# Attention tower kernel: attention tiles of 128 tokens, the 513th query and key apart on quarters of the partitions

## The chip, the cores and the metric

The kernel runs as one program on one core of a Trainium2 chip. The metric is the device time of one execution in microseconds. A profile of one execution shows when each engine worked: TensorE (PE; its weight loads are the rows PEld), VectorE (DVE), ScalarE (ACT), GpSimd (POOL) and the queues that issue transfers (SP).

## The reference, cut to what matters

The whole program is a small tower for 4 images of 513 tokens (512 and a class token) with 192 channels. Two of its layers are softmax attention with 12 heads of 16 channels; the rest (token features, a state-space mixer, MLPs, a mixture of experts, a spiking layer) is not touched by the change. For each image and head both layers compute

```python
qkv = (xp @ w_qkv).reshape(B2, N, 3, H, hd).transpose(2, 0, 3, 1, 4)   # N = 513, H = 12, hd = 16
a = jax.nn.softmax(jnp.einsum('bhnd,bhmd->bhnm', q, k) * scale, axis=-1)
o = jnp.einsum('bhnm,bhmd->bhnd', a, v)
```

513 is one more than four times 128, and 128 is the number of partitions and of TensorE rows and columns.

## The kernel before, in words

An attention layer (`attention_layer`, called for `att0` and for `att1`) has three stages: `qkv` makes queries, keys and values, `attention` does the softmax sums, `heads_out` projects. Before, 513 tokens were cut in five tiles (`KT`): four of 104 and one of 97.

`qkv` goes over 20 tiles (4 images by 5). Per tile TensorE projects queries and keys (L1817, 384 columns, float32), then values (L1822, 192 columns, float32), and turns 12 blocks of the result so that channels lie on partitions (L1839). ScalarE and VectorE split the projections in float16 parts and copy the turned blocks to `q2` and `kT`.

`attention` goes over 12 groups (4 images by 3 sets of four heads). The four heads of a group are numbered by `gi` (0, 1) and `e` (0, 1); heads with e=0 lie on partitions 0 to 63, those with e=1 on 64 to 127, so two matmuls of 64 rows can run side by side. A group needs, first, the maximum over the keys for each query:
- *scores* (L1982): 20 matmuls (2 gi, 5 tiles of queries, 2 e), each tile against 512 keys, into three PSUM banks in turn (`ring`). VectorE reduces each bank to a maximum (L2068).
- *last keys* (L1993): 10 small matmuls with the 513th key, which VectorE joins to the maxima (two operations, L2079).
- *turn* (L2004): 10 transposes that put the maxima in one row; VectorE copies the row of e=0, ScalarE that of e=1, into `q2` (L1936, two copies of 513 numbers each), where the next matmuls subtract it.

Then the softmax sums, with the keys on the partitions:
- *keys* (L2027): 20 units (2 halves of 257 queries, 5 tiles of keys, 2 gi), each a pair of matmuls (e=0 and 1) into one of two pairs of banks, and one Exp on ScalarE for each unit (L2103, 514 elements a partition).
- *values* (L2043): for each tile of keys four float32 matmuls, one for each head, side by side on quarters of 32 columns; the trace shows each as two records. ScalarE copies the sums of a half away (L2092).

TensorE's order is written by hand: a step is keys, a pair of scores, keys, and the values of two steps earlier. A group has 10 steps. The scores run `LEAD = 13` steps ahead, so those of the first group and part of the next stand alone at the start of the stage (called the fill here), and the last 13 steps have none. The last keys follow the values of the group's step 6 (counted from 0), the turn those of step 8. Waits: scores wait until the bank three places back in the ring is free; keys of unit n wait for the Exp of unit n-2; the first keys of a group wait for both engines' copies of the row.

## Time and profile before

| | us |
|---|---|
| median of 3 runs | 1756.95 (1753.33 to 1761.33) |
| the profiled execution, its own time | 1750.74 |
| its span in the trace | 1748.9 |
| PE busy / DVE busy / ACT busy | 1476.3 / 1280.7 / 1048.4 |
| attention of the first layer: fill, then the steps | 763.7 to 779.8, then to about 942.5 |
| attention of the second layer: fill, then the steps | 1408 to 1424, then to about 1588 |

The times in the rows below count from the start of the span. A busy time is the time in which an engine had at least one instruction under way. Matmuls overlap, and the records of those that run side by side start within some nanoseconds of each other, so the distance from the start of one block to the start of the next says more than a block's length.

### The profile page before, as it was taken

To read this page: it belongs to the slowest core of one execution; us is meant where nothing else is said; L and a number is where in the kernel's file an instruction comes from. 1 tells how busy PE (TensorE), PEld (TensorE's weight loads), DVE (VectorE), ACT (ScalarE), POOL (GpSimd) and SP (SyncE) were. 2 spreads that over 40 slices of the span, in tenths; PEclk is the share of its full clock that TensorE was granted. 3 is DMA by queue.
4 is the path that set the end of the run, shared out by engine and by line. 5 is a ranking of instruction groups with operands and counts; after the bars stand their busy time and mean duration, and the time that the engine had idled before them with its cause. 6 is when DMAs were issued, how large, how long until landed. Compare 5 with 4: busy or idle time off the path is not lost. (4 is left out here: it accounts for less than half of the span.)

```text
span 1748.9 us, 36641 instructions
## 1 busy us (share of the span) xinstructions
PE 1476.3 (84%) x14396; PEld 1114.7 (64%) x14396; DVE 1280.7 (73%) x2547; ACT 1048.4 (60%) x1871; POOL 414.7 (24%) x424
## 2 busy tenths in 40 slices
PE   5889998798499889899999719995697999999795
PEld 5889897697455657654445618895676744446574
DVE  5988897489789547369995757884655389994566
ACT  6998897334678264548896306664002549995565
POOL 0000000101656120359910117872001310000200
PEclk9999999699599989879999659998797979999897
DMA  5110100100000100025500732121100000000101
GB/s 146 28 42 29 37 1 20 36 1 1 7 2 2 35 1 15 1 82 170 171 16 2 210 119 61 61 62 50 48 1 14 1 1 2 2 2 2 35 1 37
DMA packets 52748, 67.96 MB, mean 39 GB/s; under 512 B 11535, under 2 KB 41489, under 8 KB 52578
## 3 DMA queue, kind: packets, MB, share of 16 engines
q1 hardware_dynamic: 46022, 50.30, 9.6%
q0 software_dynamic: 3840, 9.18, 1.8%
q10 hardware_dynamic: 2716, 6.14, 1.4%
q8 instruction: 115, 1.88, 0.4%
q14 instruction: 55, 0.45, 0.1%
HBM read 46.97 MB, written 18.65 MB: 38 GB/s over the span
## 5 line engine op out<-in xcount | busy, mean ns | idle before, releaser
L2068 DVE TENSOR_REDUCE att_max<-banks 104x1 f32<-104x512 f32 (+1 forms) x480 | 296.8, 684 | 10.2 <-PE banks L1982 6.5
L2103 ACT ACTIVATE att_p<-banks 104x514 f32<-104x514 f32 (+1 forms) x480 | 262.4, 599 | 31.4 <-PE banks L2027 19.1
L339 PE MATMUL banks<-tok_wT,feature_halves 128*128 128x192 f16 x2592 | 228.7, 248 | 23.9 <-DVE feature_halves L365 12.8
L339 PEld LDWEIGHTS banks<-tok_wT,feature_halves 128*128 128x128 f16 x2592 | 216.2, 99 | 33.2 <-DVE feature_halves L365 18.8
L2027 PE MATMUL banks<-att_q,att_kT 64*104 64x257 f16 (+1 forms) x960 | 157.1, 301 | 3.6 <-ACT att_p L2103 2.9
L2043 PE MATMUL banks<-att_p,att_v 104*32 104x257 f32 (+1 forms) x1920 | 154.8, 396 | 0.9
L1982 PE MATMUL banks<-att_kT,att_q 64*104 64x512 f16 (+1 forms) x480 | 126.9, 424 | 5.9 <-DVE att_max L2068 3.5
L2027 PEld LDWEIGHTS banks<-att_q,att_kT 64*104 64x104 f16 (+1 forms) x960 | 62.5, 121 | 107.0 <-ACT att_p L2103 80.4
L365 DVE TENSOR_TENSOR feature_halves<-features,feature_halves 128x2048 f16<-128x2048 f32 x54 | 123.4, 2286 | 6.5 <-ACT feature_halves L462 6.5
L134 PE MATMUL banks<-ones 128*128 128x256 f16 x654 | 88.5, 294 | 27.5 <-PEq L251 13.6
L462 ACT CAST feature_halves<-features 128x2048 f16<-128x2048 f32 x54 | 102.2, 1893 | 10.9 <-PE banks L339 10.1
L134 PEld LDWEIGHTS banks<-ones 128*128 128x128 f16 x654 | 65.7, 105 | 45.3 <-issue 25.3
L2828 ACT COPY slot_xT<-banks 128x512 f16<-128x512 f16 x40 | 23.4, 586 | 95.3 <-PE banks L2778 95.3
L740 POOL MEMSET xT<- 1x4104 f32 x1 | 3.5, 3518 | 312.6 <-POOLq L251 312.6
L1878 DVE TENSOR_TENSOR att_qkv_parts<-banks,att_qkv_parts 104x192 f16<-104x192 f32 (+1 forms) x80 | 25.1, 355 | 69.2 <-ACT att_qkv_parts L1858 69.2
L2791 PE MATMUL banks<-slot_xT,expert_w 128*128 128x128 f16 x1200 | 74.4, 221 | 0.2
L2807 PE MATMUL banks<-expert_w,slot_hidden_halves 128*128 128x192 f16 x720 | 66.1, 246 | 9.9 <-DVE slot_hidden_halves L2876 9.9
L354 DVE SCALAR_TENSOR_TENSOR angle_rest<-raw_T,freq,turns 128x1024 f32<-128x1024 f32 x54 | 69.1, 1280 | 6.2 <-ACT turns L239 5.7
L1982 PEld LDWEIGHTS banks<-att_kT,att_q 64*104 64x104 f16 (+1 forms) x480 | 51.5, 126 | 32.4 <-DVE att_max L2068 20.2
L2745 POOL DMA_INDIRECT slot_x<-token_rows,slot_comes x40 | 53.7, 1344 | 75.6 <-POOLq L2446 63.9
L2791 PEld LDWEIGHTS banks<-slot_xT,expert_w 128*128 128x128 f16 x1200 | 70.2, 99 | 1.8 <-issue 1.8
L1817 PE MATMUL banks<-att_qkv_w,xT 96*104 96x384 f32 (+3 forms) x160 | 65.0, 531 | 6.9 <-POOL att_qkv_parts L1793 4.4
(472 smaller groups left out, 3399.0 us busy)
## 6 DMA issues: line engine op xcount, KB each, us to landing
expert_w_in<-in_L_ffn_w_dram SPq DMA_DIRECT2D x16, 576.0 KB, 4.6
expert_w_halves<-expert_w_halves SPq DMA_DIRECT2D x32, 288.0 KB, 2.6
tok_w<-in_L_tok_W_dram ACTq DMA_DIRECT2D x4, 1152.0 KB, 7.2
expert_w2s<-expert_w_halves SPq DMA_DIRECT2D x1, 4608.0 KB
expert_y<-expert_out SPq DMA_DIRECT2D x6, 513.0 KB
expert_w1s<-expert_w_halves SPq DMA_DIRECT2D x2, 1536.0 KB
raw<-in_x_dram SPq DMA_DIRECT2D x2, 1152.0 KB, 5.4
expert_w1s<-expert_w_halves SPq DMA_DIRECT2D x3, 768.0 KB
```

The lines of the kernel that those rows point to most:

```text
L134: pe.matmul(c.bank[bank][:, 0:256], ones[:, 0:128], ones, start=True, stop=True)
L339: ins = pe.matmul(c.bank[t // 2][:, (t % 2) * D:(t % 2 + 1) * D], fh[:, s, q, z, t * 128:(t + 1) * 128], wT[:, y, k, 6 * q + wf, :], start ...
L354: own.did(dve.scalar_tensor_tensor(fr[:, n % 2, :], rT[:, k, hf * HALF:(hf + 1) * HALF], freq_col(k, f), fm[:, n % 2, :], ALU.mult, ALU.su ...
L365: dve.tensor_tensor(fh[:, s, :, 1, :], feat[:, s, :, :], fh[:, s, :, 0, :], ALU.subtract).then_inc(flow, 1)
L462: act.copy(fh[:, s, :, 0, :], feat[:, s, :, :]).then_inc(fhigh, 1)
L1982: pe.matmul(bank_of(("s", n))[0:qn, 0:KEYS], q2[r, 2 * j + gi, b * T + q0:b * T + q0 + qn], kT[r, 2 * j + gi, b * T:b * T + KEYS], start=T ...
L2027: pe.matmul(c.pair[2 + n % 2][0:kn, 512 * e:512 * e + HALF], kT[r, 2 * j + gi, b * T + k0:b * T + k0 + kn], q2[r, 2 * j + gi, b * T + STAR ...
L2043: ins = pe.matmul(acc[32 * hh:32 * hh + 32, 0:HALF], v[0:kn, b, k, h, :], p[0:kn, (n + hh // 2) % RING, hh % 2, :], start=(k == 0), stop=( ...
L2068: dve.reduce_max(mx[0:qn, n // NS % 2, 2 * gi + e, k:k + 1], bank_of(unit)[0:qn, 0:KEYS], X).then_inc(maxed, 1)
L2103: act.activation(p[0:kn, n % RING, :, :], c.pair[2 + n % 2][0:kn, :].rearrange("p (e q) -> p e q", e=2)[:, :, 0:HALF], ACT.Exp, scale=scal ...
L2791: ins = pe.matmul(ps, ws[:, s, at:at + 128], xt[:, s, b, :], start=(k == 0), stop=(k == len(TERMS) - 1))
L2807: ins = pe.matmul(ps, hh[:, s, a, f, :], w2[:, f, b, :], start=(f == k == 0), stop=(f == NF - 1 and k == 2))
```

## The change

Attention now works in tiles of 128 tokens (`AT = 4` of them for an image). The 513th token of each of the four heads in a group becomes a unit of its own, each head on its own quarter of 32 partitions:
- `qkv`: 16 tiles of 128 and one of four tokens (the last of each image). For that one the values are projected by 32 small matmuls, which repeat the last 32 tokens of an image on each quarter of the output; eight ScalarE activations keep row 31 of each quarter (`vlast`), the other rows become zero.
- `attention`: 16 scores of 128 queries, and *last queries*: four matmuls for the last query, with one reduction for all four heads. Last keys: 8 and 4 matmuls. One more small VectorE operation joins the last query with the last key, one more places it. The turn has 8 transposes and two one-column matmuls.
- The copy of the row of maxima becomes two copies: 512 numbers of float16, and one number (a cast).
- Keys: 16 full units and two for the last key (four matmuls of 32 columns side by side, one Exp of 257 elements for four heads). A step with the last key has one unit in place of two; a group still has 10 steps and ten sets of values.
- ScalarE's copies of the row come after the Exp of unit NB-3 as before, which is now unit 15 of 18 and was unit 17 of 20.

```diff
-        tiles = [(b, k) for b in range(BATCH) for k in range(len(KT))]
+
+
+        tiles = [(b, k) for b in range(BATCH) for k in range(AT)] + [None]
         N = len(tiles)
+        vlast = att.vlast
 
         def cols(n):
+            if tiles[n] is None:
+                return slice(SEQ, NT, T), BATCH
             b, k = tiles[n]
-            return b * T + KT[k][0], KT[k][1]
+            return slice(b * T + k * 128, b * T + (k + 1) * 128), 128
...
+                    if tiles[n] is None:
+                        pe.wait_ge(v_out, n)
+                        for b in range(BATCH):
+                            for hh in range(4):
+                                for o in range(2):
+                                    r = DH + o
+                                    ins = pe.matmul(c.bank[2 + b // 2][32 * hh:32 * hh + 32, b % 2 * D:(b % 2 + 1) * D],
+                                                    c.xT[0:r, o, (b + 1) * T - 32:(b + 1) * T], w[0:r, o, 2 * D:3 * D],
+                                                    start=(o == 0), stop=(o == 1))
+                        ins.then_inc(pv, 1)
+                        return
...
+                        if tiles[n] is None:
+                            act.wait_ge(init, 10)
+                            for i in range(2):
+                                for hh in range(4):
+                                    at_row = 32 * hh + 31
+                                    act.activation(vlast[:, 2 * i:2 * i + 2, :, hh, 0:HD],
+                                                   c.bank[2 + i][:, 0:2 * D].rearrange(
+                                                       "p (b j h e) -> p b j h e", b=2, j=3, h=4)[:, :, :, hh, :], ACT.Copy,
+                                                   scale=c.const("ident")[:, at_row:at_row + 1]).then_inc(v_out, 1)
...
         S_UNITS = [(gi, k, e) for gi in range(2) for k in range(NK) for e in range(2)]
         NS = len(S_UNITS)
-        PAIRS = NS // 2
-        B_UNITS = [(half, k, gi) for half in range(2) for k in range(NK) for gi in range(2)]
-        NB = len(B_UNITS)
-        LEAD = PAIRS + 3
+        SLOTS = NS // 2 + 2
+        STEPS = [[(half, k, 0), (half, k, 1)] if k < NK else [(half, k, None)] for half in range(2) for k in range(NK + 1)]
+        UNITS = [unit for step in STEPS for unit in step]
+        FIRST = [sum(map(len, STEPS[:i])) for i in range(len(STEPS))]
+        STEP_OF = [i for i, step in enumerate(STEPS) for _ in step]
...
+        for n in range(G * SLOTS + 2):
+            g, u = divmod(n, SLOTS)
+            if g < G and u < SLOTS - 2:
+                ring += [("s", g * NS + 2 * u), ("s", g * NS + 2 * u + 1)]
+            ring += [("ends", g)] if u == SLOTS - 2 else []
+            ring += [("last", g)] if u == SLOTS - 1 else []
             ring += [("max", g - 1, 0), ("max", g - 1, 1)] if u == 1 and g else []
...
+        def ends_of(g):
+
+            b = groups[g][0]
+            return slice((b + 1) * T - 32, (b + 1) * T)
...
-            copy(q2[r:r + 1, 2 * j + gi, b * T:(b + 1) * T], bank[r:r + 1, 0:T]).then_inc(mc[e], 1)
+            copy(q2[r:r + 1, 2 * j + gi, b * T:b * T + KEYS], bank.bitcast(F16)[r:r + 1, 0:KEYS]).then_inc(mc[e], 1)
+            copy(q2[r:r + 1, 2 * j + gi, b * T + KEYS:(b + 1) * T], bank[r:r + 1, KEYS - 1:KEYS]).then_inc(mc[e], 1)
...
+                def last_queries(g):
+                    b, j = groups[g]
+                    free(("ends", g))
+                    for gi in range(2):
+                        for e in range(2):
+                            r, to = slice(64 * e, 64 * e + 64), 32 * (2 * gi + e)
+                            ins = pe.matmul(bank_of(("ends", g))[to:to + 32, 0:KEYS], q2[r, 2 * j + gi, ends_of(g)],
+                                            kT[r, 2 * j + gi, b * T:b * T + KEYS], start=True, stop=True)
+                    ins.then_inc(ends, 1)
...
+                    for gi in range(2):
+                        for e in range(2):
+                            r, to = slice(64 * e, 64 * e + 64), 32 * (2 * gi + e)
+                            ins = pe.matmul(bank[to:to + 32, 4 * NK:4 * NK + 1], q2[r, 2 * j + gi, ends_of(g)],
+                                            last[r, 2 * j + gi, b, e:e + 1], start=True, stop=True)
                     ins.then_inc(lasts, 1)
...
+                            pe.transpose(bank.bitcast(F16)[:, 128 * k:128 * k + 128], mexp[:, g % 2, gi, k, :], idh[:, :])
+                        pe.matmul(bank[:, KEYS - 1:KEYS], mexp[:, g % 2, gi, NK, :], one[:, 0:1], start=True, stop=True
+                                  ).then_inc(mt, 1)
...
-                    g, u = divmod(s, PAIRS)
-                    if u == PAIRS - 1 and g < G:
+                    g, u = divmod(s, SLOTS)
+                    if u == SLOTS - 2 and g < G:
+                        last_queries(g)
+                    if u == SLOTS - 1 and g < G:
                         last_keys(g)
...
+                    if k == NK:
+                        for gi in range(2):
+                            for e in range(2):
+                                r, to = slice(64 * e, 64 * e + 64), 32 * (2 * gi + e)
+                                ins = pe.matmul(c.pair[2 + n % 2][to:to + 32, 0:HALF], kT[r, 2 * j + gi, ends_of(g)],
+                                                q2[r, 2 * j + gi, queries], start=True, stop=True)
+                        ins.then_inc(keyed, 1)
+                        return
...
+                        if k == NK:
+                            ins = pe.matmul(acc[32 * hh:32 * hh + 32, 0:HALF], vlast[:, b, j, hh, :], p[:, n % RING, 0, :],
+                                            start=False, stop=True)
+                        else:
+                            ins = pe.matmul(acc[32 * hh:32 * hh + 32, 0:HALF], v[:, b, k, 4 * j + hh, :],
+                                            p[:, (n + hh // 2) % RING, hh % 2, :], start=(k == 0), stop=False)
...
+                for t in range(G * NT_ + BEHIND):
+                    g, step = divmod(t, NT_)
+                    if g < G:
+                        keys(g, FIRST[step])
+                        scores(LEAD + t)
+                        if len(STEPS[step]) == 2:
+                            keys(g, FIRST[step] + 1)
                     if t >= BEHIND:
-                        values(2 * (t - BEHIND))
+                        values(t - BEHIND)
...
+                    elif unit[0] == "ends":
+                        g = unit[1]
+                        dve.wait_ge(ends, g + 1)
+                        dve.reduce_max(mlast[:, g % 2, 0:1], bank_of(unit)[:, 0:KEYS], X).then_inc(ends_max, 1)
...
+                        dve.tensor_tensor(mlast[:, g % 2, 1:2], mlast[:, g % 2, 0:1], bank_of(unit)[:, 4 * NK:4 * NK + 1],
+                                          ALU.max).then_inc(last_max, 1)
...
+                        dve.wait_ge(last_max, g + 1)
+                        dve.tensor_scalar(mexp[:, g % 2, :, NK, 32:128:64],
+                                          c.const("ident")[:, 31:128:32].rearrange("p (i e) -> p i e", e=2),
+                                          mlast[:, g % 2, 1:2], None, ALU.mult).then_inc(placed, 1)
...
+                    if k == NK:
+                        act.activation(p[:, n % RING, 0, :], c.pair[2 + n % 2][:, 0:HALF], ACT.Exp, scale=scale
+                                       ).then_inc(expd, 1)
+                    else:
+                        act.activation(p[:, n % RING, :, :],
+                                       c.pair[2 + n % 2][:, :].rearrange("p (e q) -> p e q", e=2)[:, :, 0:HALF],
+                                       ACT.Exp, scale=scale).then_inc(expd, 1)
...
-                    if i == 13:
+                    if i == 12:
                         copy_sums(2 * g)
```

On PE, in the first group of `attention`, steps 4 to 6. Lines of keys: L2027 before, L2106 and L2099 (last key) after; scores: L1982 and L2034; values: L2043, and L2124 and L2121 (last key) after; last keys: L1993, and L2056 and L2061; last queries: L2043 after. Before, step 4 and then step 6 with the last keys:

```order
L2027 MATMUL banks<-att_q,att_kT 97x257 x2
L1982 MATMUL banks<-att_kT,att_q 104x512 x2
L2027 MATMUL banks<-att_q,att_kT 97x257 x2
L2043 MATMUL banks<-att_p,att_v 32x257 x4
...
L2027 MATMUL banks<-att_q,att_kT 104x257 x2
L1982 MATMUL banks<-att_kT,att_q 97x512 x2
L2027 MATMUL banks<-att_q,att_kT 104x257 x2
L2043 MATMUL banks<-att_p,att_v 32x257 x4
L1993 MATMUL banks<-att_last_keys,att_q 104x2 x10
```

And now, steps 4, 5 and 6:

```order
L2099 MATMUL banks<-att_q,att_kT 32x257 x4
L2034 MATMUL banks<-att_kT,att_q 128x512 x2
L2124 MATMUL banks<-att_p,att_v 32x257 x4
L2106 MATMUL banks<-att_q,att_kT 128x257 x4
L2124 MATMUL banks<-att_p,att_v 32x257 x4
L2043 MATMUL banks<-att_kT,att_q 32x512 x4
L2106 MATMUL banks<-att_q,att_kT 128x257 x4
L2121 MATMUL banks<-att_p,att_last_values 32x257 x4
L2056 MATMUL banks<-att_last_keys,att_q 128x2 x8
L2061 MATMUL banks<-att_last_keys,att_q 32x1 x4
```

Step 4 has one block of keys in place of two; steps 5 and 6 have no scores, so that their four keys stand together.

On ACT, around the copies of the row of maxima in the first layer (sums are copied by L2092 before and L2183 after). Before:

```order
L2092 COPY att_aT<-banks 128x257
L2103 ACTIVATE att_p<-banks 104x514 x4
L1936 COPY att_q<-banks 1x513 x2
L2103 ACTIVATE att_p<-banks 97x514 x2
L2103 ACTIVATE att_p<-banks 104x514 x4
L2092 COPY att_aT<-banks 128x257
```

And now:

```order
L2183 COPY att_aT<-banks 128x257
L2198 ACTIVATE att_p<-banks 128x514 x3
L1985 COPY att_q<-banks 1x512
L1986 CAST att_q<-banks 1x1
L1985 COPY att_q<-banks 1x512
L1986 CAST att_q<-banks 1x1
L2198 ACTIVATE att_p<-banks 128x514
L2195 ACTIVATE att_p<-banks 128x257
L2198 ACTIVATE att_p<-banks 128x514 x4
L2183 COPY att_aT<-banks 128x257
```

Between the copies and the next group there are two Exps as before, of which the second has half the elements; two casts of one number have joined the copies.

## Rows read from the trace of the kernel before

**Rows 1.** The page's costliest groups: count, busy us, mean ns, idle before and releaser.

```profile
L2068 DVE TENSOR_REDUCE att_max<-banks 104x1 f32<-104x512 f32 (+1 forms) x480 | 296.8, 684 | 10.2 <-PE banks L1982 6.5
L2103 ACT ACTIVATE att_p<-banks 104x514 f32<-104x514 f32 (+1 forms) x480 | 262.4, 599 | 31.4 <-PE banks L2027 19.1
```

**Rows 2.** Engines by stretch, first attention layer: PE, PEld, DVE, ACT, POOL busy; clock, DMA, GB/s.

```profile
763.70:779.80 16.10, 14.28 (x46) 5.17 (x46) 15.33 (x28) 0.97 (x2) 11.63 (x8) 0.63 0.43 149
779.80:942.50 162.70, 160.16 (x1828) 73.32 (x1827) 145.49 (x261) 145.71 (x282) 99.21 (x46) 0.97 0.32 103
```

**Rows 3.** Timeline of PE, one group of the second layer: start us, us, instruction.

```profile
1479.37 0.32 PE L2027 MATMUL banks<-att_q,att_kT 64*104 64x257 f16 x2
1479.52 0.38 PE L1982 MATMUL banks<-att_kT,att_q 64*104 64x512 f16 x2
1479.74 0.27 PE L2027 MATMUL banks<-att_q,att_kT 64*104 64x257 f16 x2
1479.94 0.64 PE L2043 MATMUL banks<-att_p,att_v 104*32 104x257 f32 x8
1480.51 0.63 PE L2004 MATMUL banks<-att_ident,att_max_placed 104*128 104x104 f16 x10
1481.08 0.31 PE L2027 MATMUL banks<-att_q,att_kT 64*97 64x257 f16 x2
...
1482.78 0.32 PE L2027 MATMUL banks<-att_q,att_kT 64*104 64x257 f16 x2
...
1483.27 0.32 PE L2027 MATMUL banks<-att_q,att_kT 64*104 64x257 f16 x2
...
1484.09 0.32 PE L2027 MATMUL banks<-att_q,att_kT 64*104 64x257 f16 x2
...
1488.88 0.32 PE L2027 MATMUL banks<-att_q,att_kT 64*104 64x257 f16 x2
...
1491.27 0.65 PE L1993 MATMUL banks<-att_last_keys,att_q 128*104 128x2 f16 x10
1491.85 0.32 PE L2027 MATMUL banks<-att_q,att_kT 64*104 64x257 f16 x2
```

**Rows 4.** Timeline of DVE, the same group.

```profile
1478.32 0.27 DVE L2079 TENSOR_TENSOR att_max_placed<-att_max,banks 104x10 f16<-104x10 f32 x2
1481.25 0.75 DVE L1936 COPY att_q<-banks 1x513 f16<-1x513 f16 x2
1482.04 9.94 DVE L2068 TENSOR_REDUCE att_max<-banks 104x1 f32<-104x512 f32 x16
1492.02 0.28 DVE L2079 TENSOR_TENSOR att_max_placed<-att_max,banks 104x10 f16<-104x10 f32 x2
```

**Rows 5.** Timeline of ACT, the same group.

```profile
1480.95 1.06 ACT L1936 COPY att_q<-banks 1x513 f16<-1x513 f16 x2
1482.04 2.19 ACT L2103 ACTIVATE att_p<-banks 97x514 f32<-97x514 f32 x4
1484.47 1.09 ACT L2103 ACTIVATE att_p<-banks 104x514 f32<-104x514 f32 x2 [0.24 <-PE banks L2027]
```

**Rows 6.** Timeline of PE at the end of `qkv`, first layer.

```profile
756.86 1.50 PE L1817 MATMUL banks<-att_qkv_w,xT 96*104 96x384 f32 x4
758.20 0.81 PE L1822 MATMUL banks<-att_qkv_w,xT 96*104 96x192 f32 x4
758.85 0.71 PE L1839 MATMUL banks<-att_ident,att_qkv_parts 104*128 104x104 f16 x12
759.40 1.50 PE L1817 MATMUL banks<-att_qkv_w,xT 96*97 96x384 f32 x4
```

**Rows 7.** Timeline of DVE in the fill of the first layer.

```profile
764.14 12.05 DVE L2068 TENSOR_REDUCE att_max<-banks 104x1 f32<-104x512 f32 x20 [0.74 <-PE banks L1982]
```

**Rows 8.** Timeline of ACT elsewhere: a small instruction and the one after it.

```profile
693.95 0.22 ACT L680 ACTIVATE att0n_sd<-att0n_ve 114x18 f32<-114x18 f32 x1 [1.14 <-DVE att0n_ve L622]
694.08 0.53 ACT L686 ACTIVATE xN<-hN,att0n_sc 114x192 f32<-114x192 f32 x1
```

More of the change, by code:

```diff
@@ L1793, in _ @@
                 pool.memset(parts[:, :, 1, :, 32:33], -1.0).then_inc(init, 1)
+                pool.memset(att.one[:, :], 1.0).then_inc(att.set, 1)
                 for n in range(N):
@@ L1852, in _ @@
                     if n < N:
-                        b, k = tiles[n]
                         at, m = cols(n)
@@ L1946, in _ @@
             def _(pool):
-                pool.wait_ge(att.set, 3)
+                pool.wait_ge(att.set, 4)
                 for e in range(2):
@@ L2025, in keys @@
+                    k0 = b * T + 128 * k
                     for e in range(2):
                         r = slice(64 * e, 64 * e + 64)
-                        pe.matmul(c.pair[2 + n % 2][0:kn, 512 * e:512 * e + HALF],
-                                  kT[r, 2 * j + gi, b * T + k0:b * T + k0 + kn],
-                                  q2[r, 2 * j + gi, b * T + START[half]:b * T + START[half] + HALF],
-                                  start=True, stop=True).then_inc(keyed, 1)
-                def values(n):
-                    g, i = divmod(n, NB)
+                        ins = pe.matmul(c.pair[2 + n % 2][:, 512 * e:512 * e + HALF], kT[r, 2 * j + gi, k0:k0 + 128],
+                                        q2[r, 2 * j + gi, queries], start=True, stop=True)
@@ L2035, in values @@
+                    ins.then_inc(keyed, 1)
+                def values(t):
+                    g, step = divmod(t, NT_)
                     b, j = groups[g]
-                    half, k, _ = B_UNITS[i]
-                    kn = KT[k][1]
-                    pe.wait_ge(expd, n + 2)
-                    if k == 0 and n:
+                    half, k, _ = STEPS[step][0]
+                    n = g * NB + FIRST[step]
+                    pe.wait_ge(expd, n + len(STEPS[step]))
+                    if k == 0 and t:
@@ L2046, in values @@
                     ins.then_inc(summed, 1)
                 for s in range(LEAD):
-                    score_pair(s)
+                    scores(s)
                     others(s)
-                for t in range(G * PAIRS + BEHIND):
-                    if t < G * PAIRS:
-                        keys(2 * t)
-                        score_pair(LEAD + t)
-                        keys(2 * t + 1)
+                for t in range(G * NT_ + BEHIND):
+                    g, step = divmod(t, NT_)
+                    if g < G:
[3 more added lines that the diff above has]
+                            keys(g, FIRST[step] + 1)
```

122 lines of the change are left out of this document (62 added, 60 removed).

## The prediction, made before the changed kernel ran

> **What bounds the kernel now.** I read the page's costliest groups first, then the engines by stretch, then the timelines of PE, DVE and ACT over one group, and last the end of `qkv`. The change removes whole instructions of two groups at the top of the page: 480 reductions of 684 ns and 480 Exps of 599 ns [rows 1]. Whether this is worth anything depends on what paces the steps, and by stretch nothing is idle: in the 162.7 us of steps of one layer PE is busy 160.2, DVE 145.5, ACT 145.7 [rows 2]. So the group has to be taken apart.
>
> A group lasts 13.70 us, from the joining of one set of maxima to the next (1478.32 to 1492.02 [rows 4]). The reader should see three clocks that tick almost alike in it.
>
> PE: a step begins with keys at 1479.37, goes on with scores after 0.15, keys after another 0.22, values after 0.20, and ends 0.57 later: 1.14. The turn adds 0.57 (1480.51 to 1481.08), the last keys 0.58 (1491.27 to 1491.85) [rows 3]. Without waits PE would need 10 x 1.14 + 0.57 + 0.58 = 12.55, so it waits 1.15 of 13.70.
>
> DVE: 20 reductions in the fill take 12.05, that is (12.05 - 0.68) / 19 = 0.598 each [rows 7]. Twenty of them are 11.96; with two copies (0.75) and joining (0.27) [rows 4] and some 0.2 between kinds of instruction DVE needs 13.2. Two reductions a step are 1.196.
>
> ACT with PE: Exps of a pair start 0.49 apart (1.09 for two of 0.60 [rows 5]). Keys wait for the Exp two units back. An Exp starts 0.38 after its keys (1484.09 [rows 3], 1484.47 [rows 5]); the second starts 0.49 later, takes 0.60, and the keys that need its bank start 0.14 after its end (Exps from 1482.04, second end 1483.13 [rows 5]; keys 1483.27 [rows 3]). So the second keys of the next step come 0.38 + 0.49 + 0.60 + 0.14 = 1.61 after the first keys of this one, while PE alone would be there after 1.14 + 0.37 = 1.51. If both orders settle, a step lasts 1.19 to 1.20, and the two steps from 1488.88 to 1491.27 last 2.39 [rows 3]. This loop is as slow as DVE's 1.196. That is the centre of my forecast: taking work from DVE alone frees nothing in a full step.
>
> The largest wait is elsewhere. From the start of the turn to the first keys of the next group are 2.27 us (1480.51 to 1482.78 [rows 3]): 0.44 until ACT's copies start at 1480.95, 1.09 until the Exp at 1482.04 [rows 5], its 0.60, and 0.14. PE's own work there is 0.57 + 1.14 = 1.71, so 0.56 is waiting.
>
> **The change, one group.** PE's work: six full steps stay at 1.14 (6.84); 104 or 128 columns of weights make no difference to the 257 or 512 columns that stream. The two steps with the last key have one block of keys, 0.15 + 0.22 + 0.57 = 0.94, and step 5 exchanges its scores for the last queries, step 6 has none and 12 small matmuls for 10 (0.70 for 0.58). To this come changes of the array's shape. Keys before scores take 0.15, the same keys before values 0.20 [rows 3]; I put each further change at 0.05 to 0.10 and take 0.08. The last-key steps have two more (1.10 each), the last queries one (1.14 + 0.08 = 1.22), the last keys one (0.92 + 0.70 + 0.05 = 1.67). Sum: 6.84 + 2.20 + 1.22 + 1.67 + 0.57 = 12.50. PE saves 0.05 and not the 0.6 that the removed matmuls suggest.
>
> The Trainium skill, "TensorEngine Tiling (Array Packing)", Key Properties, says that a change of tiling mode, not of tile, drains the engine. It speaks against the change, which brings a mode that attention did not have (64 rows by 32 columns). By it the 0.05 to 0.10 are real; without it PE's sum would be 12.05.
>
> DVE: 17 reductions 10.17, copies 0.75 and two casts, joining 0.27 and two more small operations: about 11.8. Cast and small operations I take at 0.1 to 0.2. DVE leaves the bound; it was only one of two.
>
> ACT: 16 Exps at 0.49 and two of 257 elements; it needs less than PE throughout. But between the turn and the next group its chain grows. The second small instruction after another starts 0.13 after it [rows 8]; a last one before an Exp ends first, as the copies do (1.06 for both, next Exp at 1.09 [rows 5]). The casts thus cost 0.13 + 0.22 less the 0.11 that the last copy is no longer waited out: 0.24 (bounds 0.1 and 0.45). First keys come 0.44 + 1.09 + 0.24 + 0.60 + 0.14 = 2.51 after the turn's start. PE's work there is 0.57 + 1.10 = 1.67: 0.84 of waiting. The last-key unit with its short block falls just into this wait, so its saving is lost.
>
> The loop shows at another place. Without scores, step 6 has its second keys 0.15 after the first, but the Exp two units back ends as before: keys at 1.61 after the start of step 5, PE there at 1.22 + 0.15 = 1.37. I take 0.22, since the short Exp gave some slack. In the full steps 0.59 of waits stood before (1.15 - 0.56); those behind a short Exp fall away, and I keep 0.30. Group: 12.50 + 0.84 + 0.22 + 0.30 = 13.86, 0.16 more than now. Over 22 periods (11 in each layer) **+3.5 us**. Bounds: without shape costs (0.29 outside the wait), casts and the wait in step 6 it is 13.1, -13; four quarter matmuls one after the other at three places (+0.4) and casts at 0.45 make 14.5, +17.
>
> **Fill.** Three reductions fewer are 3 x 0.598 = 1.8, less 0.2 for small operations. But the granted clock is 0.63 over the fill, so part of it is at 1.2 GHz, and this lasts beyond its end (0.97 over the steps) [rows 2]. Steps that start earlier run at the lower clock, where I count half: 0.85 a layer, **-1.7** (bounds -3.6 and 0).
>
> **Tail.** The last 13 steps have no scores and are paced by the loop at about 1.19. The two with the last key become 0.15 + 0.08 + 0.57 = 0.8: **-1.4** for two layers (bounds -2 and 0).
>
> **`qkv`.** A tile takes 1.34 + 0.65 + 0.55 = 2.54 on PE, without a gap [rows 6]. Twenty are 50.8. The transposes stream 128 for 104 columns: 0.67. Sixteen tiles are 16 x 2.66 = 42.6; the four-token tile has 1.34, 12 transposes (0.67), and X for 32 matmuls of 192 columns. Behind them ACT has eight activations and two copies, so the stage ends some 1.15 after PE, where it ended 0.8 after it. New sum 45.8 + X for 51.6: it saves 5.8 - X a layer. A float32 matmul of 192 columns is two records of 0.16 (four in 0.65 [rows 6]). One after the other X is 10.4; if the four quarters run side by side, 2.6. The nearest row is the values: four matmuls on quarters, eight records in 0.64, side by side [rows 3]. But there each quarter has one instruction, here the two halves of a sum follow each other on one quarter before the next quarter has its turn. Then a quarter's second waits for its first and keeps back the rest, and neighbours overlap by half. I take 6: **+0.4** for both layers (bounds -6.4 and +9.2).
>
> The Trainium skill, "TensorE: Matmul & The Clock Gate", Part 3, says that matmuls start and end strictly in program order. By that rule X is between 5 and 7; the values' row does not decide it, as their records alternate by quarter.
>
> The new memsets and casts of DVE and POOL at the start of `qkv` lie beside the first tiles, where both wait for ACT.
>
> **Sum.** 3.5 - 1.7 - 1.4 + 0.4 = +0.8 on the profiled 1750.74. The median of the runs is 6.2 above that execution, so I forecast 1756.95 + 0.8, about 1757.5.
>
> **Rivals.** (A) *DVE was the bound.* Then full steps fall towards 1.14 and the waits with them: group at 12.50 + 0.6 = 13.1, or at most 13.35, -8 to -13, plus fill, tail and a cheap `qkv` (-4): about 1743. For it: DVE needs 13.2 of 13.70, the most of the three, and its reductions run on without a gap (16 in 9.94 [rows 4]). Against it: PE has the same 2.39 for two steps from the loop alone. (B) *The small matmuls of `qkv` queue.* X at 10.4 or, with weights loaded between them, 12, is 4.4 to 6 more a layer, and ACT's reads wait behind: +9 to +12 on my sum, 1768; slower by 0.5% from X = 10. For it: 32 instructions on quarters in pairs with one target. Against it: the values run side by side. (C) *The quarter matmuls of attention run in turns*, four scores of 512 columns in 0.44 or more and keys in 0.3, or the casts drain the engines: +0.3 a group, +7, 1764. (D) *Nothing of it happens on the path*: the same time, and inside my forecast.
>
> **How the numbers follow.** About 0.5%, 8.8 us, is what a measurement of this kernel tells from no change. My forecast (with D) 0.46, its own range 1749 to 1765; A 0.28; B 0.15; C 0.11, half of which lies within 0.5%. Faster 0.28, same 0.48, slower 0.24. The range takes in most of A and of B: 1741 to 1770.
>
> **What would show it.** In the profile after, a group of 13.6 to 14.0 from one joining to the next; first keys 2.5 after the turn's start; second keys of step 6 more than 0.15 after the first, with the Exp as releaser; DVE no longer without gaps. The block of 32 matmuls should last about 6. A group under 13.4 makes A right and my loop wrong; a block over 10 makes B right; last queries that take over 0.4 to the next keys make C right.

## The result, and the profile after

The changed kernel took 1737.03 us (median of four runs, 1734.35 to 1741.36), the kernel before 1758.24 beside it (1753.33 to 1761.33). The ratio is 0.9885, 95% interval 0.9858 to 0.9912: 21 us faster, where +0.8 was forecast, and below the forecast's range. The profiled execution of after took 1737.85 with a span of 1736.10. That of before was one of its quickest (1750.74 against a median of 1758.24), so the two spans differ by 12.8 only, and stages that the change doesn't touch took 7 us longer in the second (4.5 of it between the two attention layers). I therefore compare stages and not spans. By the starts of TensorE's instructions in the two traces (us):

| stretch | before, layer 1 / 2 | after, layer 1 / 2 | difference | forecast |
|---|---|---|---|---|
| `qkv`: first projection to first scores | 58.02 / 59.14 | 54.98 / 56.33 | -5.8 | +0.4 |
| fill: first scores to first turn | 14.49 / 14.49 | 13.14 / 12.75 | -3.1 | -1.7 |
| eleven groups: first to twelfth turn | 153.09 / 153.11 | 150.80 / 146.65 | -8.8 | +3.5 |
| tail: twelfth turn to last values | 14.88 / 14.88 | 13.73 / 13.73 | -2.3 | -1.4 |
| sum | | | -20.0 | +0.8 |

The signs of fill and tail were right. The two terms that miss are `qkv` and the group. First the page of after, for [rows 1]:

```profile
L2149 DVE TENSOR_REDUCE att_max<-banks 128x1 f32<-128x512 f32 x384 | 234.9, 682 | 6.9 <-PE banks L2034 5.9
L2198 ACT ACTIVATE att_p<-banks 128x514 f32<-128x514 f32 x384 | 211.9, 600 | 30.9 <-PE banks L2106 22.8
```

The counts fell by a fifth, the cost of one stayed (684 and 599 before). The fill and the steps of layer 1, with [rows 2]'s columns:

```profile
761.70:776.00 14.30, 13.21 (x47) 3.23 (x44) 13.94 (x26) 0.71 (x3) 9.57 (x6) 0.50 0.39 132
776.00:939.40 163.40, 157.03 (x1898) 60.35 (x1897) 131.54 (x275) 133.45 (x286) 101.06 (x48) 0.98 0.33 106
```

DVE lost 14.0 and ACT 12.3 us of work in a layer. TensorE's weight loads (PEld) fell from 73.3 to 60.4 us although there are more of them (1897 for 1827): that is the first sign of what the forecast missed. One group of layer 2 on PE, for [rows 3]:

```profile
1483.75 0.40 PE L2071 MATMUL banks<-att_ident,att_max_placed 128*128 128x128 f16 x4
...
1484.33 0.29 PE L2099 MATMUL banks<-att_q,att_kT 64*32 64x257 f16 x4
...
1486.13 0.29 PE L2106 MATMUL banks<-att_q,att_kT 64*128 64x257 f16 x2
...
1491.92 0.40 PE L2106 MATMUL banks<-att_q,att_kT 64*128 64x257 f16 x4
1492.25 0.64 PE L2124 MATMUL banks<-att_p,att_v 128*32 128x257 f32 x8
1492.82 0.40 PE L2043 MATMUL banks<-att_kT,att_q 64*32 64x512 f16 x4
1493.15 0.53 PE L2106 MATMUL banks<-att_q,att_kT 64*128 64x257 f16 x4
1493.61 0.64 PE L2121 MATMUL banks<-att_p,att_last_values 128*32 128x257 f32 x8
1494.18 0.35 PE L2056 MATMUL banks<-att_last_keys,att_q 128*128 128x2 f16 x8
1494.46 0.18 PE L2061 MATMUL banks<-att_last_keys,att_q 64*32 64x1 f16 x4
1494.58 0.28 PE L2106 MATMUL banks<-att_q,att_kT 64*128 64x257 f16 x2
1494.70 0.38 PE L2034 MATMUL banks<-att_kT,att_q 64*128 64x512 f16 x2
...
1495.70 0.29 PE L2106 MATMUL banks<-att_q,att_kT 64*128 64x257 f16 x2
...
1496.96 0.40 PE L2071 MATMUL banks<-att_ident,att_max_placed 128*128 128x128 f16 x4
```

The group lasts 1496.96 - 1483.75 = 13.21 (13.70 before, 13.86 forecast). The twelve small matmuls of the last keys take 0.40 (1494.18 to 1494.58), where ten took 0.58 and I had put twelve at 0.70 with 0.05 for shapes. Scores follow keys after 0.12, not 0.15, and an unimpeded full step is 1.12 (1494.58 to 1495.70). The turn's chain reaches the first keys after 2.38 (2.27 before, 2.51 forecast). Its copies on ACT, for [rows 5]:

```profile
1484.19 0.58 ACT L1985 COPY att_q<-banks 1x512 f16<-1x512 f16 x1 [0.78 <-PE banks L2072]
1484.68 0.15 ACT L1986 CAST att_q<-banks 1x1 f16<-1x1 f32 x1
1484.73 0.58 ACT L1985 COPY att_q<-banks 1x512 f16<-1x512 f16 x1
1485.21 0.15 ACT L1986 CAST att_q<-banks 1x1 f16<-1x1 f32 x1
1485.39 0.60 ACT L2198 ACTIVATE att_p<-banks 128x514 f32<-128x514 f32 x1
```

From the first copy to the Exp are 1.20 (1.09 before): the casts cost 0.11, since a small one behind a copy gives way to the next after 0.05. DVE, for [rows 4]:

```profile
1485.44 7.30 DVE L2149 TENSOR_REDUCE att_max<-banks 128x1 f32<-128x512 f32 x12
1493.27 0.69 DVE L2154 TENSOR_REDUCE att_max_last<-banks 128x1 f32<-128x512 f32 x1 [0.53 <-PE banks L2043]
...
1494.94 0.26 DVE L2167 TENSOR_TENSOR att_max_placed<-att_max,banks 128x8 f16<-128x8 f32 x2
1495.09 0.23 DVE L2169 TENSOR_SCALAR att_max_placed<-consts,att_max_last 128x4 f16<-128x4 f32 x1
```

DVE now stands idle before the last queries' reduction and again before the joining. In layer 1, for as long as GpSimd splits the experts' weights, the last of these rows reads otherwise:

```profile
843.31 0.90 DVE L2169 TENSOR_SCALAR att_max_placed<-consts,att_max_last 128x4 f16<-128x4 f32 x1
```

and the group is 13.53 there; it falls to 13.22 in the last four groups of the layer, when GpSimd is done. At the end of `qkv`, for [rows 6]:

```profile
754.18 1.46 PE L1827 MATMUL banks<-att_qkv_w,xT 96*4 96x384 f32 x4
755.48 2.87 PE L1836 MATMUL banks<-att_qkv_w,xT 96*32 96x192 f32 x64
758.28 1.23 PE L1860 MATMUL banks<-att_ident,att_qkv_parts 128*128 128x128 f16 x24
```

The block of 32 small matmuls (64 records) takes 758.28 - 755.48 = 2.80, against the 6 taken and the lower bound of 2.6.

### The profile page after: what moved, and what is told of

Same layout as the page of the kernel before. It is cut to its first block and busy times, and to the rows that moved or that the text cites. A ratio compares the mean times of both kernels' runs of the same rounds, so it can differ in the third digit from the quotient of the medians.

```text
span 1736.1 us, 36685 instructions
## 1 busy us (share of the span) xinstructions
PE 1454.7 (84%) x14444; PEld 1083.2 (62%) x14444; DVE 1240.4 (71%) x2561; ACT 1015.9 (59%) x1867; POOL 407.1 (23%) x414
## 5 line engine op out<-in xcount | busy, mean ns | idle before, releaser
L2149 DVE TENSOR_REDUCE att_max<-banks 128x1 f32<-128x512 f32 x384 | 234.9, 682 | 6.9 <-PE banks L2034 5.9
L2198 ACT ACTIVATE att_p<-banks 128x514 f32<-128x514 f32 x384 | 211.9, 600 | 30.9 <-PE banks L2106 22.8
L2124 PE MATMUL banks<-att_p,att_v 128*32 128x257 f32 x1536 | 123.5, 394 | 0.5 <-ACT att_aT L2183 0.3
L2106 PE MATMUL banks<-att_q,att_kT 64*128 64x257 f16 x768 | 112.3, 282 | 6.0 <-ACT att_p L2198 3.1
L2034 PE MATMUL banks<-att_kT,att_q 64*128 64x512 f16 x384 | 107.8, 416 | 9.8 <-PEq L1793 4.0
L2106 PEld LDWEIGHTS banks<-att_q,att_kT 64*128 64x128 f16 x768 | 36.7, 94 | 85.8 <-ACT att_p L2198 51.8
L2902 PEld LDWEIGHTS banks<-expert_w,slot_hidden_halves 128*128 128x128 f16 x720 | 58.2, 97 | 12.9 <-issue 9.8
L2840 POOL DMA_INDIRECT slot_x<-token_rows,slot_comes x40 | 46.8, 1169 | 74.5 <-POOLq L2541 62.7
L2034 PEld LDWEIGHTS banks<-att_kT,att_q 64*128 64x128 f16 x384 | 31.1, 95 | 48.8 <-DVE att_max L2149 20.5
L456 ACT ACTIVATE features<-angle_abs,half_pi 128x1024 f32<-128x1024 f32 x54 | 61.5, 1138 | 0.0
```

What stands on the lines that cost most here:

```text
L2034: pe.matmul(bank_of(("s", n))[:, 0:KEYS], q2[r, 2 * j + gi, q0:q0 + 128], kT[r, 2 * j + gi, b * T:b * T + KEYS], start=True, stop=True).th ...
L2106: ins = pe.matmul(c.pair[2 + n % 2][:, 512 * e:512 * e + HALF], kT[r, 2 * j + gi, k0:k0 + 128], q2[r, 2 * j + gi, queries], start=True, st ...
L2124: ins = pe.matmul(acc[32 * hh:32 * hh + 32, 0:HALF], v[:, b, k, 4 * j + hh, :], p[:, (n + hh // 2) % RING, hh % 2, :], start=(k == 0), sto ...
L2149: dve.reduce_max(mx[:, n // NS % 2, 2 * gi + e, k:k + 1], bank_of(unit)[:, 0:KEYS], X).then_inc(maxed, 1)
L2198: act.activation(p[:, n % RING, :, :], c.pair[2 + n % 2][:, :].rearrange("p (e q) -> p e q", e=2)[:, :, 0:HALF], ACT.Exp, scale=scale).the ...
L2902: ins = pe.matmul(ps, hh[:, s, a, f, :], w2[:, f, b, :], start=(f == k == 0), stop=(f == NF - 1 and k == 2))
```

## The experiments

The expectations speak of these theories. **W**: a weight load of exactly 128 float16 columns is quicker, and this is what the forecast left out of TensorE's work. **Loop** (L and L2 in the expectations): DVE (1.196 a step) and the loop of Exp and keys (about 1.19) pace the full steps together, so relieving one frees little. **A** (rival D there): DVE alone was the bound. **X** (F there, against Q): the order in which the small matmuls of `qkv` are issued decides whether the four quarters run side by side. **P**: the form of L2169 (one input and a scalar) makes it slow in layer 1. **S**: L2169 waits for GpSimd because all its operands lie in SBUF. Kernels whose name begins with b are edits of the kernel before, with a of the changed one. Group periods are from turn to turn in layer 2 where nothing else is said. Where a kernel ran once its single time decides nothing, and I go by the periods in its trace, nearly all of which agree within 0.03 from group to group.

**b_wide: the kernel before with 128 columns in each weight load of keys, scores and last keys** (the queries and keys padded by 32 tokens, tiles still 104; the same edit in the keys and the last keys).

```diff
-pe.matmul(bank_of(("s", n))[0:qn, 0:KEYS], q2[r, 2 * j + gi, b * T + q0:b * T + q0 + qn],
+pe.matmul(bank_of(("s", n))[0:128, 0:KEYS], q2[r, 2 * j + gi, b * T + q0:b * T + q0 + 128],
```

> The kernel before, tiles still of 104 and 97 tokens, but the scores, the keys and the last keys load 128 columns of weights (the rows beyond the tile are computed and not used). Theory W: a weight load of full 128 float16 columns is quicker (95 ns for 120 in the two traces), so the last keys fall from 0.58 to about 0.45 a group and keys before scores from 0.15 to 0.12; the group falls from 13.70 to 13.3 to 13.5. Rival D (VectorE was the bound, and its 20 reductions stay): the blocks may be shorter, the group stays at 13.6 to 13.70. Rival: the load time goes by something else that tiles of 128 bring, nothing changes at all.

**b_127: the same with 127 columns.**

```diff
-pe.matmul(bank_of(("s", n))[0:qn, 0:KEYS], q2[r, 2 * j + gi, b * T + q0:b * T + q0 + qn],
+pe.matmul(bank_of(("s", n))[0:127, 0:KEYS], q2[r, 2 * j + gi, b * T + q0:b * T + q0 + 127],
```

> As b_wide, with 127 columns of weights. Theory W, that only the full 128 columns are quick: loads of 120 ns or more, last keys at 0.58 or more, group 13.70 as before. Rival (loads get quicker gradually, or by the zero padding of the buffers): close to b_wide.

Measured: b_wide 1754.29, b_127 1764.49, the kernel before beside them 1756.54 (one run each). The groups by line of the weight loads, 1480 to 1560 us: busy us, mean ns. First the kernel before:

```profile
L2027 PEld LDWEIGHTS banks<-att_q,att_kT 64*104 64x104 f16 (+1 forms) x232 | 15.0, 119 | 24.1 <-ACT att_p L2103 17.1 <-issue 3.5
...
L1993 PEld LDWEIGHTS banks<-att_last_keys,att_q 128*104 128x104 f16 x55 | 3.1, 128 | 2.5 <-DVE att_max L2068 2.5
L2004 PEld LDWEIGHTS banks<-att_ident,att_max_placed 104*128 104x128 f16 (+1 forms) x60 | 2.9, 97 | 2.5 <-issue 2.5
```

then b_wide:

```profile
L2028 PEld LDWEIGHTS banks<-att_q,att_kT 64*128 64x128 f16 x236 | 11.9, 93 | 25.4 <-ACT att_p L2104 15.5 <-issue 6.5
...
L1994 PEld LDWEIGHTS banks<-att_last_keys,att_q 128*128 128x128 f16 x60 | 1.9, 97 | 2.5 <-DVE att_max L2069 2.5
```

and b_127:

```profile
L2028 PEld LDWEIGHTS banks<-att_q,att_kT 64*127 64x127 f16 x234 | 16.2, 130 | 23.9 <-ACT att_p L2104 17.4 <-issue 3.3
...
L1994 PEld LDWEIGHTS banks<-att_last_keys,att_q 128*127 128x127 f16 x60 | 4.0, 138 | 2.5 <-issue 2.5
```

W holds for the loads: 104 columns 119 ns, 127 columns 130, 128 columns 93. One column more takes 37 ns away. The Trainium skill, "TensorE: Matmul & The Clock Gate", Weight-path perf modes, says that the fast load is on when the number of weights is 128 and the type is not float32; these three traces agree. Yet the group of b_wide is 13.56, 0.14 less than before and outside the expected 13.3 to 13.5, and that of b_127 is 13.84, 0.14 more. TensorE's timeline in b_wide shows why so little arrives:

```profile
1480.95 0.40 PE L1994 MATMUL banks<-att_last_keys,att_q 128*128 128x2 f16 x10
1481.28 0.29 PE L2028 MATMUL banks<-att_q,att_kT 64*128 64x257 f16 x2
...
1482.74 0.29 PE L2028 MATMUL banks<-att_q,att_kT 64*128 64x257 f16 x2
```

Ten last keys take 0.33 and not 0.58, but the step behind them takes 1.46 (1481.28 to 1482.74), 0.24 more than in the kernel before: what TensorE saves it waits for one step on.

**b_dve: before, each reduction over 384 of the 512 keys**.

```diff
-dve.reduce_max(mx[0:qn, n // NS % 2, 2 * gi + e, k:k + 1], bank_of(unit)[0:qn, 0:KEYS], X
+dve.reduce_max(mx[0:qn, n // NS % 2, 2 * gi + e, k:k + 1], bank_of(unit)[0:qn, 0:384], X
```

> The kernel before, with reductions over 384 of the 512 keys: the maxima leave out a quarter of the keys. Each reduction is about 0.13 shorter, VectorE needs 10.6 for 13.2 in a group. Theory L (ScalarE and TensorE pace the full steps at 1.19 by themselves): 13.5 to 13.70. Rival D (VectorE was the bound): 12.9 to 13.2.

**b_exp: before, each Exp over 2 x 200 of 2 x 257 elements**.

```diff
-act.activation(p[0:kn, n % RING, :, :],
-               c.pair[2 + n % 2][0:kn, :].rearrange("p (e q) -> p e q", e=2)[:, :, 0:HALF],
+act.activation(p[0:kn, n % RING, :, 0:200],
+               c.pair[2 + n % 2][0:kn, :].rearrange("p (e q) -> p e q", e=2)[:, :, 0:200],
```

> The kernel before, with Exps over 200 of the 257 queries of each half: 57 columns a head stay at a constant 0.5 set once at the start. Each Exp is about 0.12 shorter. Theory L: the wait of the second keys goes and so does 0.12 of the turn's chain, but VectorE's 1.196 a step comes right behind, so 13.4 to 13.6. Rival D: only the turn's chain gains, 13.6 to 13.70.

**b_cut2: both edits in the kernel before; a_cut2: both in the changed one.**

> The kernel before, with reductions over 384 of 512 keys and Exps over 200 of 257 queries at once (both parts left out as before). Alone they gave 13.61 and 13.50 for 13.70. Theory L2 (two loops of almost the same period, one through VectorE and one through ScalarE, hold the full steps; TensorE's own work is 12.55): together far more than the sum, 12.8 to 13.1. Rival (they add up, TensorE is what is left): 13.4.

> The changed kernel with the same two parts left out (reductions of the full tiles over 384 keys, Exps over 200 of 257 queries). TensorE's own work, from its blocks in the changed kernel, is about 12.1 a group (six full steps of 1.12, two of 1.12, 1.23, 1.30, turn 0.58). Theory L2: 12.3 to 12.6, so that about 0.4 of the 0.48 by which the change shortened the group is TensorE's. Rival (the gain came from VectorE's and ScalarE's fewer units alone): no shorter than b_cut2.

Measured: b_dve 1747.71 and b_exp 1751.80 (before beside them 1756.54), b_cut2 1736.33 and a_cut2 1727.59 (before 1755.93), one run each. A reduction became 553 ns instead of 684, an Exp 502 instead of 599. The groups are 13.61, 13.50 and 13.19: -0.09 for DVE alone, -0.20 for the Exps alone, -0.51 for both, more than the two together (0.29), though 13.19 lies above the 12.8 to 13.1 expected. Most of b_dve's gain lies in the fill (11.93 for 14.49), where DVE does pace. In b_cut2 most full steps run at TensorE's own 1.14 to 1.15; one of those below takes 1.23, and the step behind the turn still takes 1.61:

```profile
1485.48 0.32 PE L2030 MATMUL banks<-att_q,att_kT 64*104 64x257 f16 x2
...
1486.62 0.32 PE L2030 MATMUL banks<-att_q,att_kT 64*104 64x257 f16 x2
...
1487.85 0.32 PE L2030 MATMUL banks<-att_q,att_kT 64*104 64x257 f16 x2
...
1488.99 0.31 PE L2030 MATMUL banks<-att_q,att_kT 64*97 64x257 f16 x2
...
1490.13 0.32 PE L2030 MATMUL banks<-att_q,att_kT 64*104 64x257 f16 x2
```

A falls as a cause of its own (it needed b_dve at 12.9 to 13.2), and the loop theory holds in kind: two clocks nearly alike, and TensorE close behind both. In a_cut2 the group is 12.78 in layer 2, not the 12.3 to 12.6 expected: in the changed kernel the two cuts are worth another 0.44. With both engines relieved the two kernels still differ by 0.41 (13.19 and 12.78), where TensorE's own work differs by 0.48 as worked out below. So the rival that fewer maxima and Exps alone made the gain falls. While GpSimd works in layer 1 it stays at 13.53, so there something else paces (below).

**a_quarter: the changed kernel, with the small matmuls of `qkv` issued quarter by quarter** instead of going round the quarters.

```diff
-for b in range(BATCH):
-    for hh in range(4):
+for hh in range(4):
+    for b in range(BATCH):
```

> The changed kernel; the 32 matmuls of the last values in qkv stand quarter by quarter (eight in a row on one quarter of 32 columns), not image by image. In the changed kernel the block took 2.80 where I had put 6. Theory Q (each quarter has its own deep queue): 2.8 to 3.2 again. Rival F (few instructions may wait for a busy quarter, so the order in the program counts): 5 to 11.

Measured: 1754.45, one run (before 1756.53, the changed kernel 1737.03 in its own runs). The block, same 64 records of the same length:

```profile
755.59 8.75 PE L1836 MATMUL banks<-att_qkv_w,xT 96*32 96x192 f32 x64
764.27 1.23 PE L1860 MATMUL banks<-att_ident,att_qkv_parts 128*128 128x128 f16 x24
```

8.68 us instead of 2.80, in F's range and not in Q's. The stretch to the first scores is 60.85 and 62.20 in the two layers, 5.87 longer in each, and nothing of it is hidden. These 11.7 us are what the traces show of the single run's 17.4; the rest lies in no stretch that the edit touches. Only the order of two loops differs, so X holds: the quarters run side by side when they come in turn (2.80 against 2.6), even with two float32 matmuls of a sum behind each other on one quarter. The records of the changed kernel show how: the first halves of the sums (96 rows) of all four quarters start between 755.48 and 755.70, and no second half (97 rows) starts before 755.80, although the program has that of the first quarter in second place.

**a_tt: L2169 as a tensor_tensor; a_late: ACT's row copies one unit later; a_both: both.**

```diff
-dve.tensor_scalar(mexp[:, g % 2, :, NK, 32:128:64],
+dve.tensor_tensor(mexp[:, g % 2, :, NK, 32:128:64],
                   c.const("ident")[:, 31:128:32].rearrange("p (i e) -> p i e", e=2),
-                  mlast[:, g % 2, 1:2], None, ALU.mult).then_inc(placed, 1)
+                  mlast[:, g % 2, 1:2].unsqueeze(2).broadcast_to((128, 2, 2)), ALU.mult
+                  ).then_inc(placed, 1)
...
-if i == NB - 3 and g + 1 < G:
+if i == NB - 2 and g + 1 < G:
```

> The changed kernel, with the last query's maximum placed by a tensor_tensor against a broadcast column in place of the tensor_scalar (same numbers). In the first layer, while GpSimd splits the expert weights, that operation took 0.90 for 0.23 and the group 13.53 for 13.22. Theory P (this form of VectorE instruction waits for GpSimd's): the groups of the first layer fall to 13.22, -2 to -3 us in all. Rival (the transfers, or any VectorE write at that place, is what waits): 13.53 stays.

> The changed kernel, with ScalarE's copies of the row of maxima after the Exp of unit 16 and not 15. That Exp has its keys before the turn. Theory C (the first keys of the next group wait for the Exp that stands behind the copies): the stretch from the turn's start to these keys falls from 2.39 to 2.0 to 2.15, where the scores that wait for VectorE's copy and TensorE's own work end; the group falls to 12.9 to 13.0, -5 to -7 us. Rival (the copies come 0.2 later and VectorE's copies decide anyway): 13.2 stays.

> a_tt and a_late together. If both theories hold: group 12.9 to 13.0 in both layers, -7 to -10 us against the changed kernel, about 0.983 of the kernel before. If only one holds, 0.985 to 0.987.

Measured against the kernel before (1756.53): a_tt 1737.01, ratio 0.9879 [0.9851, 0.9908]; a_late 1738.87, 0.9916 [0.9894, 0.9938]; a_both 1737.34, 0.9889 [0.9868, 0.9909]. None can be told from the changed kernel's 0.9885, and a_both missed both ratios that were expected. In a_tt the instruction reads in layer 1

```profile
841.58 0.70 DVE L2169 TENSOR_TENSOR att_max_placed<-consts,att_max_last 128x4 f16<-128x4 f32 x1
```

and its five in 790 to 865 us have a mean of 556 ns (171 in layer 2); the group there is still 13.52. P falls. What else could hold it at one value is seen on GpSimd, here in the changed kernel:

```profile
834.29 3.13 POOL L2487 TENSOR_SCALAR expert_w_in<-expert_w_in 128x1152 f32<-128x1152 f32 x1
837.49 1.15 POOL L2489 CAST expert_w_halves<-expert_w_in 128x1152 f16<-128x1152 f32 x1
838.72 2.38 POOL L2491 TENSOR_TENSOR expert_w_halves<-expert_w_in,expert_w_halves 128x1152 f16<-128x1152 f32 x1
841.06 3.13 POOL L2487 TENSOR_SCALAR expert_w_in<-expert_w_in 128x1152 f32<-128x1152 f32 x1
```

One round of its three instructions is 6.77 us (834.29 to 841.06), two are 13.53 or 13.54: nearly every group of layer 1 lasts as long, to 0.02, in the changed kernel, in a_tt, a_late, a_both and a_cut2. The one group of 13.66 in the changed kernel holds the one round of 6.88. L2169 of 843.31 ends at 844.21, and GpSimd's 3.13 from 841.06 at 844.19; in the other groups the two ends lie as close. In a_tt L2169 ends 0.2 before GpSimd's instruction each time. The first group of layer 1 holds the longest one:

```profile
787.34 2.62 DVE L2169 TENSOR_SCALAR att_max_placed<-consts,att_max_last 128x4 f16<-128x4 f32 x1
```

It ends with GpSimd's 3.12 from 786.80. So the group is locked to GpSimd's rounds, whatever else is made shorter.

a_late cuts the turn to first keys from 2.38 to 2.20 (2.0 to 2.15 was expected), and the following four steps grow from 4.67 to 4.82: a net 0.04 of 13.22. C's group of 12.9 to 13.0 is not reached; this is the same giving back as in b_wide. With both edits (a_both) the group of layer 2 is 13.12.

**a_stt: L2162 and L2169 as one instruction that reads one operand straight from PSUM; a_stt_late: that and a_late's edit.**

```diff
-dve.tensor_tensor(mlast[:, g % 2, 1:2], mlast[:, g % 2, 0:1], bank_of(unit)[:, 4 * NK:4 * NK + 1],
-                  ALU.max).then_inc(last_max, 1)
...
-dve.wait_ge(last_max, g + 1)
-dve.tensor_scalar(mexp[:, g % 2, :, NK, 32:128:64],
-                  c.const("ident")[:, 31:128:32].rearrange("p (i e) -> p i e", e=2),
-                  mlast[:, g % 2, 1:2], None, ALU.mult).then_inc(placed, 1)
+dve.scalar_tensor_tensor(mexp[:, g % 2, :, NK, 32:128:64],
+                         bank_of(unit)[:, 4 * NK:4 * NK + 1].unsqueeze(2).broadcast_to((128, 2, 2)),
+                         mlast[:, g % 2, 0:1],
+                         c.const("ident")[:, 31:128:32].rearrange("p (i e) -> p i e", e=2),
+                         ALU.max, ALU.mult).then_inc(placed, 1)
```

> The changed kernel, with the joining and the placing of the last query's maximum in one scalar_tensor_tensor that reads its wide operand from PSUM; the numbers are the same. In the first layer the placing took 0.90 (as a tensor_scalar) and 0.70 (as a tensor_tensor) for 0.23 while GpSimd worked, and both read SBUF alone. Theory S (a VectorE instruction with all operands in SBUF waits for GpSimd's instruction, one with an operand in PSUM does not): groups of the first layer fall from 13.53 to 13.1 to 13.2, about -3 us. Rival (the write into that tile waits): 13.5 stays.

> a_stt with ScalarE's copies of the row of maxima after the Exp of unit 16. a_late alone gave 0.04 a group, since VectorE's chain of 12 reductions starts at the same time after the turn. Theory S with that: 13.05 to 13.15 in both layers, a further 1 us below a_stt.

Measured against the kernel before (1755.93): a_stt 1731.91, ratio 0.9848 [0.9829, 0.9868]; a_stt_late 1729.12, 0.9823 [0.9798, 0.9848], the quickest version by its median of all that leave nothing out. Their intervals overlap with each other, and a_stt's with that of the changed kernel, so what each edit is worth is read from the traces. The new instruction in layer 1, beside GpSimd's:

```profile
837.63 0.23 DVE L2166 SCALAR_TENSOR_TENSOR att_max_placed<-banks,att_max_last,consts 128x4 f16<-128x4 f32 x1
```

0.23, as long as the old one takes in layer 2: no waiting. The group of layer 1 falls from 13.53 to 13.15 and layer 1 from first scores to last values from 177.67 to 172.47; layer 2 from 173.14 to 172.52. In a_stt_late the group is 13.11 in both layers. The lock is gone, and S holds: the form without a PSUM operand was held up beside GpSimd, in two kinds of instruction, and the one with it was not. L2162 of the changed kernel, a tensor_tensor that reads PSUM and stands just before, says the same: 156 ns in both layers. The Trainium skill, "SBUF — State Buffer", SBUF: two separate sides, says that a VectorE instruction with two SBUF inputs, or in a mode that uses both ports, and a GpSimd instruction lock each other out of a shared pair of ports; the 0.70 of the tensor_tensor and the 0.23 agree, and the 0.90 of the tensor_scalar does if it ran in such a mode, which no run shows. Whether the port or something else is the cause no run here separates.

## Why the prediction was wrong

**What was read rightly.** No single engine set the pace: b_dve and b_exp alone move a group by 0.09 and 0.20. The turn is the largest wait, and the last-key unit falls into it. The last queries' step was put at 1.22 and took 1.23, in part by luck, since its last queries stand behind the values and not in the place of the scores (0.33 + 0.57 + 0.33); the last-key step at 1.10 and took 1.12. The new shapes of the array did cost about what I took. Two reductions a step at 0.598 stand in the traces as they did.

**The step that failed in the group: "104 or 128 columns of weights make no difference".** I looked at what streams, where that is true, and not at the loads. From it came "10 small matmuls 0.58, so 12 are 0.70". They take 0.40. With durations read from after, TensorE's own work in a group is: six full steps of 1.12 (6.72), two last-key steps of 1.12 (2.24), 1.23 for the last queries' step, 0.33 + 0.57 + 0.40 = 1.30 for step 6, 0.58 for the turn: 12.07. I had 12.50, the kernel before 12.55. So TensorE's work fell by 0.48 of the 0.49 by which the group fell; the forecast had 0.05. Of the 0.43 between them 0.35 are the last keys and the rest the full steps. A row that warned of this stood in the trace of before: the turn's weights (L2004), 128 columns, loaded in 97 ns while the keys' 104 took 119.

**The waits.** In total they stayed, 13.21 - 12.07 = 1.14 against 1.15 before; I had 1.36. The turn chain is 0.13 shorter than forecast (casts 0.11 and not 0.24), and the wait within the keys of step 6 is 0.13 and not 0.22 (values follow 0.46 after them, where four keys alone take 0.33). That the waits did not grow is not free. In b_wide the same loads took about as much from TensorE (10 x 0.03 + 0.25 = 0.55) and the group gave back all but 0.14. The change also takes three of twenty reductions from each group, and of ACT's 20 x 0.60 = 12.0 in Exps leaves 16 x 0.60 + 2 x 0.38 = 10.4, and b_cut2 shows that both have to be relieved before a step can end sooner. So neither half suffices: shorter loads alone give 0.14, and shorter reductions without shorter Exps 0.09. What fewer maxima and Exps give together without the fast loads was tried in the kernel before only through shorter instructions (b_cut2), not through fewer; that split stays open.

**Rival A** had the nearest number (1743, group 13.1 to 13.35) by a mechanism that b_dve excludes as the only one.

**The step that failed in `qkv`: "neighbours overlap by half", X = 6.** It is 2.80, at the lower bound. The rule of the Trainium skill that matmuls start and end strictly in program order, "TensorE: Matmul & The Clock Gate", Part 3, gave 5 to 7 here by my working and doesn't describe this block; a_quarter shows that order does matter, but for which quarters are supplied at once, and in the records first halves start ahead of a second half that precedes them in the program. With X at 2.8 my sum gives -3.0 a layer, and -3.04 and -2.80 were measured. Inside it misses cancel: the way from the last transposes to the first scores took 2.02 and not 1.15. Against it, the last two sets of twelve transposes took 1.23 and not 1.34. The last tile before took 3.49 from its projection to the end of its transposes (759.40 to 762.89), where my old sum has 1.34 + 0.65 + 0.55 + 0.55 = 3.09. And the first three tiles of a layer took 12.79 and 14.14 where they had taken 13.13 and 14.23, although each has 0.12 more work.

**Fill and tail** had the right sign and were too small. The fill gave -3.1 for -1.7: DVE paces it, and 1.35 and 1.74 of its three reductions' 1.8 arrived, of which I had given half to the lower clock. The steps behind it did not pay for that: the period from first to second turn went from 16.11 to 14.60 in layer 2, 1.0 more than the others gained. There the lower clock ended 7.7 us after the first turn and not 10.1 as before; no run separates this from the rest of the edit. The tail gave -2.3 for -1.4, outside its bounds. In b_wide the fast loads alone shorten it by 0.21 a layer, 0.4 of the 0.9 missing; the other half stays open. The granted clock fell to 0.50 (1.2 GHz) for about 20.5 us in each layer, before as after (767.8 to 788.2 and 1412.9 to 1433.4; 761.8 to 782.3 and 1403.5 to 1424.0).

**What I had not thought of: GpSimd.** The new L2169 stands beside GpSimd's splitting in layer 1 and costs 0.31 a group there, and 1.9 in the first (16.70, in a_stt 14.81), where it took 2.62. Without it layer 1 is as quick as layer 2.

In sum: 3.5 + 8.8 = 12.3 us of the miss are the groups, 6.2 `qkv`, 2.3 fill and tail.

## What to carry to other kernels

Compare weight loads by their column count before calling a wider tile free: full 128 columns of float16 load quicker than 104, and the small matmuls that are all load gain most. Where two engines pace a step nearly alike, an edit that relieves one shows almost nothing, and one that relieves both shows more than the two alone (0.51 against 0.29 here), so cost them together and not one by one. Issue small matmuls on quarters of the array in turn over the quarters, and where a small VectorE instruction stands beside a busy GpSimd and one of its operands comes from PSUM anyway, let it read that operand there.

## What the runs showed of the hardware that I had not expected

- Loads of float16 weights: 93 ns at 128 columns, 119 at 104, 130 at 127 (64 rows); 97, 128 and 138 with 128 rows. Two-column matmuls follow each other after about 0.035 us with 128 columns of weights and 0.058 with 104.
- 32 float32 matmuls of 192 columns on quarters: 2.80 us going round the quarters, 8.68 quarter by quarter. Going round, matmuls on other quarters start ahead of one that precedes them in the program.
- A VectorE instruction of 4 elements a partition with all operands in SBUF: 0.23 us alone (0.17 as a tensor_tensor), and beside GpSimd's mostly 0.78 to 0.90, once 2.62; with one operand in PSUM 0.23 in both places.
- A one-element cast behind a 512-element copy costs 0.05 us on ACT and 0.07 on DVE when another copy follows.
